# A Swin block in float32 on one core: the load of x moves from SyncE to GpSimd, and the residual's bias add to the front of GpSimd's step

## The reference

```python
y = _ln(x, norm1_g, norm1_b)
y = jnp.roll(y, (-SS, -SS), axis=(1, 2))
yw = y.reshape(B, nWh, WS, nWw, WS, C).transpose(0, 1, 3, 2, 4, 5).reshape(B * nW, N, C)
q, k, v = (yw @ qkv_w.T + qkv_b), split into 16 heads
attn = softmax(q * scale @ k.T + relative position bias + shift mask)
o = (attn @ v) @ proj_w.T + proj_b
x = x + jnp.roll(windows put back(o), (SS, SS), axis=(1, 2))
h = _ln(x, norm2_g, norm2_b)
h = jax.nn.gelu(h @ fc1_w.T + fc1_b, approximate=False) @ fc2_w.T + fc2_b
return x + h
```

## Time and profile before

| what | value |
| --- | --- |
| median of 3 runs | 4084.6 us (4084.42 to 4090.56) |
| the profiled execution, its own time | 4095.41 us |
| its span in the trace | 4093.6 us |
| TensorE busy | 3947.3 us (96%) |
| VectorE, ScalarE, GpSimd busy | 2855.1, 2674.9, 2002.3 us |
| one step in the steady state | about 31 us |

### The profile page before, as it was taken

One profiled execution on the slowest core, in us unless ns is written; L12 is line 12 of the kernel. 1 busy time (PEld: TensorE's weight loads), 2 busy tenths in 40 slices (PEclk: granted clock), 3 DMA queues, 4 the chain that ended last, 5 costly groups with the idle time before them and its releaser, 6 DMA issues. The chain is left out here.

```text
span 4093.6 us, 168809 instructions
## 1 busy us (share of the span) xinstructions
PE 3947.3 (96%) x72080; PEld 3111.1 (76%) x72080; DVE 2855.1 (70%) x7453; ACT 2674.9 (65%) x3712; POOL 2002.3 (49%) x3476
## 2 busy tenths in 40 slices
PE   3899999999999999999999999999999999999998
PEld 2677777777777777777777777777777777777776
DVE  6677677677767777776776776777777667677764
ACT  1666666666666666666766666666666666666664
POOL 4454545445455454544544544454454445445453
PEclk8999999999999999999999999999999999999999
DMA  2333333333333333333333333333333333333332
GB/s 77 100 108 115 109 109 112 110 105 112 114 106 110 113 111 110 111 113 105 112 114 105 110 114 110 109 111 108 108 109 117 106 109 112 112 105 109 112 109 60
DMA packets 609568, 441.49 MB, mean 108 GB/s; under 512 B 142083, under 2 KB 608371, under 8 KB 608819
## 3 DMA queue, kind: packets, MB, share of 16 engines
q1 hardware_dynamic: 608355, 428.88, 35.6%
q0 software_dynamic: 464, 1.81, 0.2%
HBM read 106.14 MB, written 51.46 MB: 38 GB/s over the span
## 5 line engine op out<-in xcount | busy, mean ns | idle before, releaser
L589 DVE TENSOR_REDUCE neg_max<-ps 113x16 f32<-113x784 f32 x1024 | 995.9, 973 | 760.7 <-PE ps L741 760.5
L421 ACT ACTIVATE probs<-ps 113x784 f32<-113x784 f32 x1024 | 844.6, 825 | 858.4 <-PE ps L776 855.7
L821 PE MATMUL ps<-w,hid 128*112 128x128 f32 x7168 | 933.5, 279 | 1.9 <-ACT hid L438 1.0
L821 PEld LDWEIGHTS ps<-w,hid 128*112 128x112 f32 x7168 | 818.4, 177 | 81.9 <-issue 79.4
L776 PE MATMUL ps<-st_q,st_k 128*49 128x196 f16 x8192 | 696.2, 249 | 0.0
L771 PE MATMUL ps<-bias,eye_k 106*64 106x392 f16 x4096 | 686.5, 331 | 0.0
L438 ACT ACTIVATE hid<-ps,col 128x784 f32<-128x784 f32 x512 | 468.1, 915 | 165.4 <-PE ps L805 144.2
L741 PE MATMUL ps<-mx_k,mx_q 128*49 128x196 f16 x8192 | 544.2, 253 | 31.7 <-DMA mx_q<-q_hi 20.0
L350 POOL TENSOR_SCALAR ve<-mv 112x7 f32<-112x7 f32 x256 | 54.4, 212 | 1048.4 <-DVE mv L527 903.1
L776 PEld LDWEIGHTS ps<-st_q,st_k 128*49 128x49 f16 x8192 | 446.9, 105 | 122.0 <-issue 0.5
L372 POOL TENSOR_SCALAR r_hi<-sums 128x98 f16<-128x98 f32 x128 | 36.5, 285 | 897.9 <-DVE sums L630 897.9
(11 more groups left out here) (109 smaller groups left out, 6502.4 us busy)
## 6 DMA issues: line engine op xcount, KB each, us to landing
st_k<-k_hi SPq DMA_DIRECT2D x256, 196.0 KB
st_q<-q_hi SPq DMA_DIRECT2D x1024, 49.0 KB
oT_raw<-pv_sb SPq DMA_DIRECT2D x256, 196.0 KB, 3.6
x_in<-in_x SPq DMA_DIRECT2D x224, 196.0 KB
x_res<-in_x SPq DMA_DIRECT2D x224, 196.0 KB
out_y<-y_out SPq DMA_DIRECT2D x224, 196.0 KB
mx_k<-k_hi SPq DMA_DIRECT2D x512, 49.0 KB
mx_q<-q_hi SPq DMA_DIRECT2D x128, 196.0 KB
```

The source lines that it names most:

```text
L421: nc.scalar.activation(probs[0:KP, w % 4, :].rearrange("p (b c) -> p b c", b=2), ps[0:KP, b:b + 2, 0:HB * WT], ACT.Exp).then_inc(s_exp, 1)
L589: nc.vector.tensor_reduce(neg_max[0:KP, :, :, w].rearrange("p e g -> p g e"), ps[0:KP, 0:2, :].rearrange("p b (g c) -> p (b g) c", g=2)[:, ...
L821: last = mm(ps[0:TP, 7, (i - first) * C:(i - first + 1) * C], hid[:, c, i * TP:(i + 1) * TP], w_2[:, c, :], start=(c == 0), stop=(c == CH ...
```

## The change

SP no longer loads x. GpSimd issues the same DMAs, the first one ahead of everything else in its program. In a step it first adds the bias to x_res (which now stands ahead of the split of the reciprocals instead of behind it), then waits for the transposes of the tile before and issues the load, and then goes on as before. The waits are the same as before, on other engines' lists.

```diff
         @block.sync
         def _(sp):
-            band_dmas(sp, xr, x_in, 0, False, False, s_x)
...
                     for im in range(2):
                         sp.dma_start(sums[:, im, :], pv_sb[2 + im:C:32, :, :]).then_inc(s_sum_dma, 16)
-                n = t + 2
-                if exists(n) and n != 0:
-
-                    sp.wait_ge(s_t1, n)
-                    band_dmas(sp, xr, x_in, n, edge(n), False, s_x)
...
         @block.gpsimd
         def _(pool):
+            band_dmas(pool, xr, x_in, 0, False, False, s_x)
...
                 n = t - 1
                 if exists(n):
 
+                    if n == 0:
+                        pool.wait_ge(s_w, 16 * N_W)
+                        pool.wait_ge(s_init, 2)
+                    pool.wait_ge(s_xres_dma, loads(n, edge(n)))
+                    nc.gpsimd.tensor_tensor(x_res[:, :, :], x_res[:, :, :],
+                                            proj_b[:, :].unsqueeze(1).to_broadcast([TP, WS, C]),
+                                            ALU.add).then_inc(s_xres, 1)
+                n = t + 2
+                if exists(n) and n != 0:
+
+                    pool.wait_ge(s_t1, n)
+                    band_dmas(pool, xr, x_in, n, edge(n), False, s_x)
+                n = t - 1
+                if exists(n):
+
                     pool.wait_ge(s_rsum, n + 1)
...
                     nc.gpsimd.tensor_scalar(r_lo[:, :, :], sums[:, :, :], LOW_SCALE, 0.0,
                                             ALU.mult, ALU.add).then_inc(s_r_lo, 1)
-                    if n == 0:
-                        pool.wait_ge(s_w, 16 * N_W)
-                        pool.wait_ge(s_init, 2)
-                    pool.wait_ge(s_xres_dma, loads(n, edge(n)))
-                    nc.gpsimd.tensor_tensor(x_res[:, :, :], x_res[:, :, :],
-                                            proj_b[:, :].unsqueeze(1).to_broadcast([TP, WS, C]),
-                                            ALU.add).then_inc(s_xres, 1)
```

## The result

The changed kernel takes 4303.5 us (median; 4292.6 to 4319.0) beside 4087.6 us for the kernel before: a ratio of 1.0521, 95% interval 1.0495 to 1.0547. So it is slower, by five times what was forecast: 216 us instead of 44, and above the upper end of the range, 4235. The profiled execution took 4292.6 us, with a span of 4290.8; the span before was 4093.6, so 197 us are to be found in the two traces.

A forecast was written before the change was run, and what follows sets the result against it. TensorE, busy 96% of the span, was taken as the bound, with x_in's landing setting its value projections. Lateness 50, edge +5, SP -8, start +1 gave +48, cut to +44: 4129 us on the median, range 4045 to 4235.

The forecast's parts named there:

- The place and the sign: x_in's landing sets TensorE's value projections; the change makes it land later, so the kernel gets slower, by 44 us.
- From the last row to the landing: Time from GpSimd's last x_in issue row until the data lands: 3.9 us, against 3.48 on SP.
- The issue: GpSimd's two x_in rows start about 0.1 us after the transposes, take 0.7 us each, end with SP's.
- the 0.4 us of lateness: x_in lands at 2008.45 instead of 2008.05 in the steady step; over 125 steps this costs 50 us.
- The price of lateness: Late x_in costs TensorE microsecond for microsecond at the value projections; 0.1 us of lateness is worth 12.5 us.
- the 125 of the sum: Number of steps with the x_in load, by which the lateness per step is multiplied: 0.4 x 125 = 50 us.
- SP's -8 us: Without x_in rows SP issues later loads earlier, mostly in edge steps, shortening TensorE's wait for mx_q by 8 us.
- +5 for the edge steps: In the 16 edge steps, later x_res and four GpSimd issue rows cost 0.3 us a step more, 5 us.
- +1 for the start: Two more GpSimd rows ahead of the memsets delay the set-up by 1.4 us, once: +1 us.
- Issuing goes by the piece: Rival: GpSimd's issue takes 1.75 us a row, x_in lands 2 to 2.8 us late, 4335 to 4435 us; chance 0.10.
- The early start: Rival: short rows and GpSimd's earlier issue land x_in by 2007.2, mostly removing the waits, 4040 to 4076 us; chance 0.27.
- VectorE's CAST: Rival: a 0.31 us CAST on VectorE blocks GpSimd's second x_in issue each step, +39 us, 4168 us; chance 0.06.

The follow-up runs named there:

- e1: Kernel before with only the bias add moved to the front of GpSimd's step, x_in still loaded by SP: ratio 0.9988.
- e10: Changed kernel with oT_raw's two loads cut to one row of 256 bytes each from tile 1 on: 4097.5 us, ratio 1.0025.
- e3: Changed kernel, but SP issues oT_raw only once GpSimd has issued both x_in DMAs: 4158.7 us, ratio 1.0169.
- e2: Kernel before with only the x_in load moved to GpSimd, bias still added behind r_lo: 4309.7 us, ratio 1.0541.
- e8: Changed kernel with the x_in load split, GpSimd issuing image 0 and SP image 1 ahead of oT_raw: 4100.1 us, ratio 1.0022.
- e4: Kernel before with SP issuing oT_raw ahead of x_in instead of behind it, no x_in load on GpSimd: 4222.0 us, ratio 1.0315.
- e11: Kernel before with oT_raw's two loads cut to one row of 256 bytes each from tile 1 on: 4073.6 us, ratio 0.9962.
- e12: Changed kernel with five unused matmuls added ahead of the last fc1 chunk to fill TensorE's wait: 4258.9 us, ratio 1.0411.
- e6: Changed kernel with a second x_in tile, GpSimd's load bringing the tile of the step after next: 4056.0 us, ratio 0.9912.

## Where the prediction was right, and which step failed

**The place and the sign** were right. x_in's landing sets the value projections, lateness is paid by TensorE about microsecond for microsecond, and VectorE waits 374.7 us for x_in in place of 201.8. The bias add is hidden, as said (e1), r_hi is not held up, and SP's wait for r_lo went up from 33.5 to 186.4 us as its rows vanished. VectorE before, then VectorE and SP after:

```profile
DVE st L521 <- DMA x_in<-in_x: 201.8, 128, 2.8
```

```profile
DVE st L524 <- DMA x_in<-in_x: 374.7, 128, 5.3
SPq L273 <- POOL r_lo L388: 186.4, 127, 4.3
```

**The step that failed is "From the last row to the landing"**: 3.9 us were taken, 4.56 it was in the step above (3089.90 - 3085.34), against 3.48 on SP. The text named oT_raw's earlier issue, and that the two loads would share a stretch, as one more thing against x_in, but gave it no price of its own: it went into the rounding between 2.7 and 4.2, ends taken from two smaller loads at the start of the program. The runs show it the other way round. The price of GpSimd's queue, for which the term was made, is nothing in this term: without oT_raw's data the way takes 3.1 us on GpSimd and 3.3 on SP. oT_raw's data beside x_in's is the main price: with it x_in lands 1.47 us later on GpSimd (e10 against after), and e3, which only puts oT_raw behind x_in again, takes 145 of the 216 us away. The rows for it were there: oT_raw issued right behind x_in and full DMA engines.

**The issue** was undersized too. The rows of the changed kernel take 0.78 us in the mean (224.6 us for 288), 0.81 in the step above, where 0.7 was taken, and the first starts 0.30 us after the transposes, not 0.1. The last row ends 0.41 us later than SP's, not as early. The sentence of the Trainium skill, "DMA: Bandwidth & Descriptors" (Anatomy of one DMA), that many descriptors can be emitted before the incremental cost shows up, does not carry from 128 to 392 pieces here: 0.57 us became 0.81. The two x_in rows at the start of the changed program, 1.00 and 0.78 us beside 0.54 to 0.60 for the single loads behind them, are longer too; whether the number of pieces does it was not tried apart. In the sum the 0.4 us of lateness should have had 0.43 more from the issue (1.91 for 1.48) and 0.66 more from the landing (4.56 for 3.9): 1.49, as in that step.

**The price of lateness** lacked a term. The waits grew by 163.6 us for 1.43 us of lateness, 114 us for each microsecond, near the 125 of the sum. But a longer wait also sent TensorE to half clock: 26 places, another 50 us, at 1.43 us (32 in e2, at 1.41); 10 at 1.09; none in e8, at 0.22. e3 has 4, at 0.33, and e10 has 2, but three of those four and both of those two stand right behind a pause of GpSimd's, where TensorE waited 2.4 to 3.1 us. The prediction has no term for the clock; the kernel before never leaves 2.4 GHz in the steady state.

**The credits.** SP's -8 us is not confirmed. The wait for mx_q fell from 20.0 to 5.4, but in e4, where SP issues every row as before, it fell to 8.7, so most of that goes with the lateness. With x_in early and SP's rows gone it is 12.7 (e10), against 16.8 with them (e11): some 4 us. The +5 for the edge steps and +1 for the start were not measured apart.

**The rivals.** "Issuing goes by the piece" gave 4335 or more and was wrong in its mechanism, though its time lay nearer than the forecast. The early start did not win: 0.14 us were gained at the first issue (0.30 for 0.44 us behind the transposes) and lost to the rows. VectorE's CAST does not lengthen the second row: from 200 to 3600 us it runs beside 98 of 104 of them, and their median is 0.77 us with it and without it. The first rows take 0.84, and the cause of that is open.

## What to carry to other kernels

A load in a queue is not only behind the work ahead of it, it is also ahead of the work behind it: before it is moved to another engine, look at what that queue issues next and whether it moves data at the same time. On another engine's queue the load loses that place, and here the two transfers then ran side by side: give the other one a price of its own, and add what a longer wait does to TensorE's clock, from the stretch in which the wait falls. Where a load has a deadline inside the step, try a second buffer that removes the deadline: here it was worth more than any place of the issue that was tried, and with it the slower transfer no longer mattered.

## What the runs showed that had not been expected

In the place shown above TensorE fell to half clock behind a stretch in which it still worked 1.46 of 3.40 us and its longest single wait was 1.56 us; filling the wait with matmuls whose results nobody uses made the kernel faster by 1.0% (4303.5 to 4258.9 us).

In three of the changed kernel's steady steps GpSimd paused for 4.0 to 4.5 us between its two x_in rows, and x_in landed 2.0 to 2.4 us later still. The timeline of one:

```profile
1742.57 0.84 POOL L206 DMA_DIRECT2D x_in<-in_x  x1 [1.82 <-PE ps L849]
1747.43 0.77 POOL L206 DMA_DIRECT2D x_in<-in_x  x1 [4.02 <-issue]
```

The profile names no releaser for it; with four shorter ones ahead of a step's first row such idle time comes to 24.1 us in 7 places of the whole run. The pauses go by the count of issues and not by time: in all five runs in which GpSimd issues both x_in rows into the one tile (after, e2, e3, e10, e12) they stand ahead of the same three rows, the 38th, 108th and 178th, and last 3.3 to 5.0 us. In e10 the value projections of these three steps start 2.9 to 3.6 us later than in the median step, 9.5 us of its 24. With two tiles (e6) no pause between two rows is longer than 1.0 us. Their cause stays open.
